# Attention with two exact row maxima per key block: the order of twelve row-tiled matmuls

## The reference, cut to what matters

```python
qkv = (tokens @ w_proj + b_proj).reshape(B, N, NUM_HEADS, 3 * HEAD_DIM)
q, k, v = jnp.split(qkv, 3, axis=-1)
attn = jnp.einsum('bihd,bjhd->bijh', q, k) * SCALE
attn = jax.nn.softmax(attn, axis=2)          # over the keys j
res = jnp.einsum('bijh,bjhd->bihd', attn, v).reshape(B, N, NUM_HEADS * HEAD_DIM)
out = res @ w_out + b_out + tokens
```

## Time and profile before

| what | us |
|---|---|
| median of 3 runs | 1120.28 |
| the profiled execution | 1123.22 |
| its span | 1121.5 |
| PE weight loads busy | 482.0 (43%) |
| DVE busy | 880.7 (79%) |
| ACT busy | 787.3 (70%) |
| POOL busy | 323.7 (29%) |

### The profile page before, as it was taken

The page is one execution under the profiler, slowest core; times in us unless marked ns, Lnnn a source line. Parts: engine busy times, 40 slices in busy tenths (PEclk is TensorE's granted clock), DMA queues, the critical chain, the costliest instruction groups (busy, mean ns, idle before and its releaser), DMA issues. The chain is left out here.

```text
span 1121.5 us, 23624 instructions
## 1 busy us (share of the span) xinstructions
PE 1064.6 (95%) x7976; PEld 482.0 (43%) x7984; DVE 880.7 (79%) x1975; ACT 787.3 (70%) x1693; POOL 323.7 (29%) x384
## 2 busy tenths in 40 slices
PE   5999999999999999999999999999899997899994
PEld 2122323333232333323323333332366776899993
DVE  4999989988988988898899899994177785654446
ACT  2277877877878877888878788788666644655553
POOL 4041031113105103210410410006324565675550
PEclk7599999999999999999999999999999896999996
DMA  4417004303500710440260053000060112223318
GB/s 123 94 42 164 4 1 132 77 8 80 130 2 12 178 20 1 114 96 1 58 152 2 1 147 43 2 2 20 10 179 18 37 34 71 70 78 83 86 39 302
DMA packets 58635, 76.09 MB, mean 68 GB/s; under 512 B 15464, under 2 KB 33896, under 8 KB 58520
## 3 DMA queue, kind: packets, MB, share of 16 engines
q1 hardware_dynamic: 53368, 63.67, 23.6%
q0 software_dynamic: 4320, 8.89, 2.4%
q10 hardware_dynamic: 832, 2.03, 0.5%
HBM read 47.64 MB, written 26.65 MB: 66 GB/s over the span
## 5 line engine op out<-in xcount | busy, mean ns | idle before, releaser
L738 DVE TENSOR_REDUCE neg_half<-slot 128x1 f32<-128x512 f32 x1024 | 643.8, 682 | 73.1 <-PE slot L519 67.9
L651 ACT ACTIVATE probs<-ring 128x512 f32<-128x512 f32 x1024 | 542.0, 600 | 140.0 <-PE ring L528 139.7
L528 PE MATMUL ring<-stack_q,stack_k 50*128 50x512 bf16 (+1 forms) x2048 | 418.1, 381 | 1.3 <-issue 1.3
L519 PE MATMUL slot<-stack_k,stack_q 48*128 48x512 bf16 x1024 | 378.9, 391 | 14.6 <-DMA stack_q<-parts_dram 10.1
L562 PE MATMUL acc<-probs,v_sb 128*32 128x512 f32 x2048 | 272.8, 605 | 0.0
L528 PEld LDWEIGHTS ring<-stack_q,stack_k 50*128 50x128 bf16 (+1 forms) x2048 | 117.7, 94 | 270.9 <-issue 232.4
L519 PEld LDWEIGHTS slot<-stack_k,stack_q 48*128 48x128 bf16 x1024 | 96.0, 94 | 147.5 <-DVE neg_half L738 84.8
L1666 ACT ACTIVATE mask<-bank,w_of 128x128 f32<-128x128 f32 x284 | 81.1, 369 | 55.9 <-PE bank L1632 55.9
L437 POOL CAST m_parts<-neg_max 128x16 bf16<-128x16 f32 x32 | 6.3, 198 | 327.6 <-DVE neg_max L744 327.6
L1605 POOL DMA_INDIRECT rows_tok<-mask,x_in x71 | 68.9, 970 | 57.0 <-DVE mask L1700 52.1
L1632 PE MATMUL bank<-xt,w_of 128*128 128x128 f32 x568 | 78.0, 281 | 5.2 <-DVE w_of L1690 3.3
(11 more groups left out here) (168 smaller groups left out, 1017.9 us busy)
## 6 DMA issues: line engine op xcount, KB each, us to landing
parts_dram<-parts SPq DMA_DIRECT2D x30, 384.0 KB, 4.9
stack_k<-parts_dram SPq DMA_DIRECT2D x32, 192.0 KB, 3.9
stack_q<-parts_dram SPq DMA_DIRECT2D x64, 96.0 KB, 3.8
x_in<-rows_in SPq DMA_DIRECT2D x71, 64.5 KB, 2.2
xp<-in_x SPq DMA_DIRECT2D x8, 512.0 KB, 5.0
stack_k<-parts_dram SPq DMA_DIRECT2D x32, 128.0 KB, 3.5
xr<-in_x SPq DMA_DIRECT2D x8, 512.0 KB, 3.7
out<-zt SPq DMA_DIRECT2D x16, 256.0 KB, 2.1
```

The lines of the kernel that those rows point to most:

```text
L519: return pe.matmul(out[:, :], queries(u, BB, q % 2, ht)[rows, qt * P:(qt + 1) * P], stack_k[u % STACK_BUFS][rows, BB, ht, half * HALF:(hal ...
L528: return pe.matmul(out[:, :], stack_k[s % STACK_BUFS][rows, run, ht, kt * P:(kt + 1) * P], queries(s, run, half, ht)[rows, :], start=run = ...
L651: act.activation(probs[:, j % PROBS, h, :], ring[n % S_BANKS][:, :], ACT.Exp).then_inc(s_empty[n % S_BANKS], 1)
L738: dve.tensor_reduce(neg_half[q % 2][:, half, k:k + 1], slot[n % M_BANKS][:, :], AX.X, ALU.max, negate=True).then_inc(m_empty[n % M_BANKS], 1)
```

## The change

Two lines change. The two maxima of a half stand together, in round 1 and in round 6, and the four rounds between them hold scores alone, part A of both tiles and then part BB of both tiles. No matmul is added or removed, and none changes its tile, shape or data. Every table derived from the list (bank numbers, counts of semaphores, DVE's order) is worked out from it again. The orders of ACT (s0, s1, s2, s3) and of the jobs stay; DVE reduces M0 a, M1 a, M0 b, M1 b in place of M1 a, M0 a, M1 b, M0 b.

```diff
-FRONT = (("score", 0, A), ("max", 1, 0)), (("score", 0, BB), ("score", 1, A)), (("max", 0, 0), ("score", 1, BB))
-REAR = (("score", 2, A), ("max", 1, 1)), (("score", 2, BB), ("score", 3, A)), (("max", 0, 1), ("score", 3, BB))
+FRONT = (("max", 0, 0), ("max", 1, 0)), (("score", 0, A), ("score", 1, A)), (("score", 0, BB), ("score", 1, BB))
+REAR = (("score", 2, A), ("score", 3, A)), (("score", 2, BB), ("score", 3, BB)), (("max", 0, 1), ("max", 1, 1))
```

## The result

The changed kernel took 1136.7 us (median of 4 runs, 1134.88 to 1138.38), the kernel before 1122.8 us beside it. The ratio is 1.0118, 95% interval [1.0081, 1.0155]: slower by 13 us. The forecast was 1125.7 us in a range to 1134, with 12% for slower by over 1%. It was wrong in size. The sign was right.

What follows compares the result with a forecast made beforehand. Plain blocks were taken as bound by a PE-DVE circle through three banks (2.50 us), side-job blocks by PE. Terms 3.5 + 0.4 + 0.9 + 0.6 = 5.4 on 1120.3 gave 1125.7 us, range 1117 to 1134.

Steps and rivals of the forecast that it cites:

- The circle in a plain block: Plain blocks: round 6 waits until DVE empties the first maximum's bank; block length stays 2.50 us.
- The 0.13 and 0.14 us left over in plain blocks: Plain blocks: slack before round 1's second maximum (0.13) and next block's s3 A (0.14) need their banks; no cost.
- This rival (8%): Round 1: its pair of maxima waits for DVE, holding every score; 1150 us with 0.1 beyond; chance 8%.
- the opened circle (5%): Plain blocks: DVE runs at its own pace, PE's 2.42 us becomes the bound; 1115.7 us; chance 5%.
- `back`, 3.5 us: Blocks with a back job: s3 A waits 0.23 us for s0's ring bank, 15 times; 3.5 us.
- the rival without it (10%): Side-job blocks: the ring bank wait isn't there and only the DVE pieces stay; 1122 us; chance 10%.
- `bias`, 0.4: The one block with the bias job: s3 A's ring bank comes later, pv at 79.93 against 79.50; 0.4 us.
- `out`, 0 by 0.05: Blocks with an out job: ring bank free at 428.66, wanted at 428.71; no cost, by 0.05 us.
- The tail, 0: Last 13 blocks, without maxima: eight score matmuls already take four rounds of two; nothing gained, 0.
- The rival of the strict order (3%): Last 13 blocks: with strict program order, four steps replace five, 0.22 us each; 1122.8 us; chance 3%.
- `proj` and `v` are longer; `oturn` uses no ring bank. No cost: Blocks with proj, v or oturn side jobs: no added wait for a ring bank; 0 us.
- The start, 0.9 + 0.6 us: Two rounds of scores behind late maxima: 0.44 us each behind two solos (0.9); second block at half clock (0.6).

Runs made afterwards that it cites:

- e4: Kernel before with only the new rear (s2 and s3 scores together, both maxima in round 6), old front: 1127.2 us.
- e3: Kernel before with only the new front (both maxima in round 1, s0 and s1 scores together), old rear: 1128.0 us.
- e7: Changed kernel with the rear's first maximum in round 5 beside s3 BB, and s2 BB in round 6: 1135.9 us in one run.
- e10: Changed kernel, but with the old rear in blocks that have a side job other than mturn: 1130.3 us.
- e6: Changed kernel plus extra transposes, 24 ahead of the first maxima and one behind each solo maximum ahead of block 0: 1153.4 us.
- e5: Kernel before plus extra transposes, 24 ahead of the first maxima and one behind each solo maximum ahead of block 0: 1140.1 us.
- after: The changed kernel itself, in its first measurement against the kernel before: 1136.7 us.
- e1: The changed kernel run again with no edit: 1136.4 us, ratio 1.0095 to the kernel before.
- e9: Kernel before with the new order in blocks 0 to 3 alone, the old one in the other 252: 1130.2 us.
- e8: Kernel before with the new order only in blocks from 4 on without a side job other than mturn: 1122.8 us, ratio 0.9996.
- e2: Changed kernel with the old order in blocks 0 to 3, the new one in the other 252: 1131.9 us.

## Why the prediction was wrong, step by step

- **The circle in a plain block: right.** Round 6 waits for f0's bank and the block lasts 2.49 us. That it is 0.01 shorter was not foreseen and is worth 0.7 us over all.
- **The 0.13 and 0.14 us left over in plain blocks: right.** Round 1 doesn't wait for DVE. This rival (8%) is out. So is the opened circle (5%), which asked for 2.42. PE's wait for DVE, which was to stay near 85 us, reads 128.3; 72.1 of that is idle time that stood under another name before.
- **`back`, 3.5 us: right,** 3.1 measured; the wait was forecast as 0.23 and is 0.22, and the rival without it (10%) is out. The fifteenth block lies where no maxima are left and loses nothing, which the sum didn't see.
- **`bias`, 0.4: right,** 0.43. **`out`, 0 by 0.05: right,** the 30 blocks got 0.1 us shorter in all. **The tail, 0: right,** the 14 intervals there changed by 0.03 us in sum. The rival of the strict order (3%) wanted 2.9.
- **"`proj` and `v` are longer; `oturn` uses no ring bank. No cost": the step that failed.** I checked these blocks for the ring bank alone. f2's move from round 4 to round 6 was checked only in a plain block ("Nothing starves"), where DVE has work until 402.58. In a side block DVE is already idle, and f2's move delays the end of its work by 0.44. And "when DVE is late, f0 is late too and drags round 6" was taken as equal before and after, though the lateness itself had grown. The runs showed in its place a loss of 4.2 us in these blocks, which comes with the rear alone (4.5 in e4, 0.0 in e3), halves where f2 is moved halfway (e7) and is gone with the old rear (e10). The missing term is +4.2, and 0.25 in one block more. The rows for it were there: the timeline of DVE at an oturn block, and ahead of it.
- **The start, 0.9 + 0.6 us: the second step that failed.** Measured were 5.5 to 6.1. The 0.9 for the two `solo` jobs was right at 2.4 GHz (0.43 each, e6 and the third block of the changed kernel). The 0.6 for the second block was too small: the scores of block 0, which had filled PE's waits, all came behind the maxima, and 1.4 us were lost up to the first pv. The largest part, 3.2 to 3.8 us, stood in no term: the clock rose later and fell back. I took the clock as given by the trace of before. Why it does so is not settled; e5 and e6 show only that more work for PE did not raise it.

With 4.4 and about 4.3 added, the sum of 5.4 becomes 14.1, against 12.6 to 13.2 us of changed places measured in the table. Most of the difference is the plain blocks' small gain and the 0.4 that `back` was taken too high.

## What to carry to other kernels

When instructions are regrouped, check each queue's slack not in the steady block but in the blocks with extra work, and follow the engine that feeds on the result until it has caught up: 0.44 us of idle time moved ahead of a busy stretch of DVE became 0.42 us of PE. Don't carry the clock of one trace over to a kernel whose waits at the start change: here the longer time at 1.2 GHz cost about 3.2 us where two rounds behind each `solo` cost 0.9, and filling the waits with other work did not win it back. Where a loss adds up from places, subtract two traces block by block; here that separated four terms of 0.4 to 5.5 us in a single pair of traces.

## What the runs showed of the hardware

- The granted clock fell back to 1.2 GHz, behind maxima at DVE's pace with gaps between them, at 59 to 61 us in all six kernels that had the new front in blocks 0 to 3 and whose clock had risen by then (after, e1, e3, e7, e9 and e10); the kernel before, e4, e5 and e8, with the old front in blocks 0 to 4, had no such fall. e2, whose new fronts begin with block 4, had one at 66.7, and e6, whose clock rose at 70.3, had one at 83.9: both where a new front follows a `solo`. What exactly lets the clock fall is not shown.
- Full-array transposes between row-tiled matmuls are dear at 1.2 GHz: the pace of the maxima went from 0.60 to about 0.93 us (e5, DVE busy 7.3 of ten us with reductions of 0.68), and the clock stayed at 1.2 GHz for 51.2 us though PE was shown as busy all the time from 30 us on.
- Pairs of matmuls that fill two banks while DVE reads a third cost its reductions nothing: 682 ns on average before and after.
